# One core, cross-attention and a three-block feed-forward: first-layer weights with their output mean taken out, biases seeded into PSUM, the last layer written by token

## The chip, the core and the metric

The kernel runs on one core of one Trainium2 chip. The metric is the device time of one execution in microseconds; the time of a kernel is the median of its runs. The core has five engines that run their own queues of instructions in order and meet only at semaphores: TensorE (PE; its weight loads are listed as PEld), VectorE (DVE), ScalarE (ACT), GpSimd (POOL) and SyncE (SP, which issues the DMAs).

## The reference

`x` and `ctx` are 128 x 64 tokens of 128 features, so 8192 tokens in all. Cut to what matters:

```python
x = x + xattn(ctx, ctx, layernorm(x))        # 16 heads; softmax over the heads
h = layernorm(x)
for blk in range(3):
    i0, i1 = 2 * blk, 2 * blk + 1
    y = h @ W[i0].T + b[i0]                   # W = dequantised weights + lora_b @ lora_a
    y = (y - mean(y)) * rsqrt(var(y) + 1e-5) * gamma[blk] + beta[blk]
    y = gelu(y)
    h = y @ W[i1].T + b[i1] + h
x = x + h
```

All of it is in float32.

## The kernel before

**Two parts.** The tokens are cut into 16 chunks of 512, each four tiles of 128 tokens. The attention part walks over the chunks (`chunks`, about the first 265 us). The feed-forward part is a pipeline over the same chunks (`steps`): step `t` works on up to eight chunks at once, each at another stage. Steps 0 to 4 are placed by hand into the last chunks of the attention part (`EARLY`), steps 5 to 22 follow it; steps 8 to 13 are a loop of two steps per turn.

**Two layouts.** A first layer (`first_layer`, v = 1, 2, 3 for the three blocks) takes the transposed residual `h[v-1]` (feature by token) as weights, four tiles, and writes its output by token (token by feature), so that the mean and variance of a token lie along the free axis. A second layer takes `g[v-1]` (feature by token) and writes by feature again.

**One step, by engine.** In this order on each queue:

- PE: first layer 3 of chunk t-6 into `bank[0]`; transposes of `z[3]` of chunk t-7; first layer 2 of chunk t-4 into `bank[1]`; first layer 1 of chunk t-2 into `bank[5]` or `bank[2]`; transposes of `z[2]`, `z[1]` and of `z[0]`; second layers 3 (`bank[6]`), 2 (`bank[3]`) and 1 (`bank[4]`); transposes of `h[3]` back to by-token. Each first layer begins with `bias_rows` (L830), one bfloat16 matmul of 512 columns that writes the bias row.
- DVE: `bn_stats` of first layer 3 (L583) and `combine` of its group (group 0, with the statistics of the input chunk); `bn_stats` of first layers 2 (L591) and 1 (L595) and `combine` of group 1; `bn_stats` of the next input chunk (L570); `h[3]`, `h[2]`, `h[1]` = second layer + bias column + old h (L612, in this order); the last add into `x_all` (L618), which frees the bank and lets SP store the chunk.
- POOL: `rs2` = (variance) to the power -1/2 for group 0 and then for group 1 (L409), each followed by `nmr2` = -mean x rs (L412); then `z[0]` of chunk t in two passes (L430, L435).
- ACT: gelu of v = 3, 2, 1 (L761) on the transposed banks; `normalise(3)`, `normalise(2)` (L751, four activations of 128 columns each, from PSUM to `z[v]`); `h[0]` (L773), a copy of the transposed `z[0]`; `normalise(1)`.

`combine` (L503 to L517) has six small operations in three groups with a wait between them; `normalise` waits for `nmr2` of its group. The value that ends a step's part is its counter: `p_y[v]` first layer done, `p_st[b]` variance ready, `p_rs[b]` root ready, `p_z[v]` normalised, `p_h[v]` residual ready, `p_out` bank and chunk done.

In the start-up (chunk -1) the weights are formed as `w_eff` (L500) on DVE, transposed on PE (L823) and copied to `lin_t` on ACT (L640). Attention uses the same PSUM: `bank[4]` is `att_ps`, `bank[5]` is `wo_ps`. L557 adds the attention's output to `x_all`; one of them (chunk 14) stands on DVE's queue right behind step 4, and the bias row and the 16 matmuls of the last output projection (L830, L836 into `wo_ps`) wait for it.

## Time and profile before

| | |
|---|---|
| median of 3 runs | 407.47 us (407.38 to 407.8) |
| the profiled execution, its own time | 406.81 us |
| its span in the trace | 405.0 us |
| mean granted clock of TensorE | 0.983 |
| busy: PE / DVE / ACT / POOL | 366.2 / 351.3 / 290.1 / 288.0 us |

The profile describes one execution. The span runs from the first to the last instruction; what lies around it is 1.8 us here. Busy time on PE counts pipelined matmuls, whose ends are modelled. Instructions on DVE and ACT overlap a little: the distance from one start to the next is what an instruction costs in a queue that never waits, and its duration is what a waiting engine sees.

### The profile page before, as it was taken

The numbers are of one execution on the slowest core, as the hardware profiler recorded it, in microseconds if no ns is written. First come the engines' busy times: TensorE is split into PE (matmuls) and PEld (weight loads), VectorE is DVE, ScalarE is ACT, GpSimd is POOL, SyncE is SP. The second block draws the span as 40 slices with busy tenths as digits, with TensorE's granted clock in tenths as the row PEclk, the third lists the DMA queues.
The fourth block names the chain that finished last, engine by engine and source line by source line (L and its number), as shares of the span: only waits on it lengthen the run. The fifth ranks groups of instructions, "written<-read, shape, count | busy, mean of one in ns | idle before, by whom it ended". The sixth has DMA issues, their size and how long they took to land.

```text
span 405.0 us, 11901 instructions
## 1 busy us (share of the span) xinstructions
PE 366.2 (90%) x4205; PEld 258.1 (64%) x4205; DVE 351.3 (87%) x863; ACT 290.1 (72%) x542; POOL 288.0 (71%) x349
## 2 busy tenths in 40 slices
PE   2778999999999999999989777788999999999964
PEld 1334566677667766776656556566877887787631
DVE  4746999999999999999999999878999999888852
ACT  3447887888788878787766534358888888888741
POOL 5681998789878987898797878757667766744320
PEclk9999999999999999999999989999999999999995
DMA  5636765476547654675444100000000010001011
GB/s 164 181 105 210 218 199 150 141 235 186 159 133 221 203 159 136 201 213 163 144 133 147 39 2 2 1 2 2 28 28 26 26 52 26 28 27 53 27 53 52
DMA packets 53120, 43.26 MB, mean 107 GB/s; under 512 B 4496, under 2 KB 46944, under 8 KB 53088
## 3 DMA queue, kind: packets, MB, share of 16 engines
q1 hardware_dynamic: 53088, 42.84, 35.2%
q8 instruction: 19, 0.31, 0.3%
q14 instruction: 13, 0.11, 0.1%
HBM read 26.05 MB, written 16.78 MB: 106 GB/s over the span
## 4 chain that ended last, share of the span: by engine, by line
PE 67%; DVE 15%; POOL 7%; issue 6%; ACT 3%; DMA 1%; POOLq 0%; ACTq 0%; DVEq 0%
PE score_ps L973 8%; PE att_ps L938 7%; PE score_ps L869 7%; PE score_ps L878 6%; PE wo_ps L836 6%; PE work L1020 4%; DVE negmax L529 3%; DVE zsum L550 3%; PE score_ps L1020 3%; PE work L894 3%; PE att_ps L1020 3%; PE work L907 2%; PE score_ps L966 2%; PE score_ps L830 2%; PE work L898 2%
## 5 line engine op out<-in xcount | busy, mean ns | idle before, releaser
L373 POOL TENSOR_TENSOR probs<-probs,rz 128x1024 f32<-128x1024 f32 x64 | 136.4, 2141 | 34.0 <-DVE rz L553 33.6
L409 POOL TENSOR_TENSOR rs<-ve,minus_half 128x8 f32<-128x8 f32 (+1 forms) x40 | 55.6, 1390 | 53.4 <-DVE ve L516 53.4
L529 DVE TENSOR_REDUCE negmax<-score_ps 128x64 bf16<-128x1024 f32 x64 | 76.1, 1189 | 7.7 <-PE score_ps L869 7.6
L659 ACT ACTIVATE probs<-score_ps 128x1024 f32<-128x1024 f32 x64 | 65.6, 1025 | 23.5 <-PE score_ps L878 23.1
L550 DVE TENSOR_REDUCE zsum<-probs 128x64 f32<-128x1024 f32 x64 | 77.5, 1211 | 5.6 <-ACT probs L659 5.0
L751 ACT ACTIVATE z<-score_ps,nmr,rs 128x128 f32<-128x128 f32 x160 | 60.4, 469 | 15.3 <-POOL nmr L412 15.1
L836 PEld LDWEIGHTS wo_ps<-wo_t,att_t 128*128 128x128 f32 x256 | 37.5, 193 | 13.8 <-issue 12.2
L938 PE MATMUL att_ps<-probs,v_diag 128*32 128x64 f32 x2048 | 43.9, 225 | 1.4 <-POOL probs L373 1.4
L878 PE MATMUL score_ps<-negmax,ident_bf 128*128 128x512 bf16 x128 | 39.2, 388 | 5.6 <-DVE negmax L529 5.5
L973 PEld LDWEIGHTS score_ps<-lin_t,h 128*128 128x128 f32 x320 | 42.1, 192 | 1.3
L973 PE MATMUL score_ps<-lin_t,h 128*128 128x128 f32 x320 | 42.1, 275 | 0.0
L869 PE MATMUL score_ps<-q_stack,k_stack 128*64 128x256 f16 x512 | 40.4, 280 | 0.5 <-ACT probs L659 0.3
L938 PEld LDWEIGHTS att_ps<-probs,v_diag 128*32 128x32 f32 x2048 | 33.1, 109 | 11.5 <-issue 2.5
L836 PE MATMUL wo_ps<-wo_t,att_t 128*128 128x128 f32 x256 | 39.1, 278 | 0.0
L553 DVE RECIPROCAL rz<-zsum 128x64 f32<-128x64 f32 x64 | 35.4, 553 | 2.2
L869 PEld LDWEIGHTS score_ps<-q_stack,k_stack 128*64 128x64 f16 x512 | 23.2, 110 | 12.2 <-issue 9.7
L669 ACT ACTIVATE xln<-x_all,nmr,rstd 128x128 f32 (+1 forms) x64 | 26.2, 483 | 5.5 <-POOL rstd L399 5.5
L761 ACT ACTIVATE g<-score_ps,cols 128x512 f32<-128x512 f32 x25 | 20.0, 799 | 9.4 <-PE score_ps L966 9.4
L1020 PE MATMUL work<-g,lin_t 128*128 128x512 f32 x36 | 20.0, 638 | 3.0 <-ACT g L761 3.0
L761 ACT ACTIVATE g<-att_ps,cols 128x512 f32<-128x512 f32 x16 | 12.5, 780 | 11.5 <-PE att_ps L966 11.5
L612 DVE SCALAR_TENSOR_TENSOR h<-work,cols,h 128x512 f32<-128x512 f32 x18 | 13.4, 744 | 7.3 <-PE work L1020 7.2
L737 ACT ACTIVATE v_diag<-work 64x512 f32<-64x512 f32 x32 | 18.8, 586 | 1.1 <-PE work L907 0.7
(152 smaller groups left out, 727.6 us busy)
## 6 DMA issues: line engine op xcount, KB each, us to landing
q_parts<-parts SPq DMA_DIRECT2D x16, 512.0 KB, 3.6
q_stack<-q_parts SPq DMA_DIRECT2D x64, 128.0 KB, 2.8
k_stack<-k_parts SPq DMA_DIRECT2D x32, 256.0 KB, 3.3
ctx_sb<-in_ctx SPq DMA_DIRECT2D x16, 256.0 KB, 3.7
k_parts<-parts SPq DMA_DIRECT2D x16, 256.0 KB, 2.7
out<-x_all SPq DMA_DIRECT2D x16, 256.0 KB, 2.3
x_all<-in_x SPq DMA_DIRECT2D x14, 256.0 KB, 3.9
x_all<-in_x SPq DMA_DIRECT2D x1, 512.0 KB, 5.0
```

The lines of the kernel that those rows point to most:

```text
L373: nc.gpsimd.tensor_tensor(e[:, :, :, :], e[:, :, :, :], by_query.broadcast_to([P, BANDS, SEQ, ADJ]), ALU.mult).then_inc(s_probs, 1)
L409: nc.gpsimd.tensor_tensor(rs2[b][:, lo:hi], ve2[b][:, lo:hi], minus_half[:, lo:hi], ALU.pow).then_inc(p_rs[b], 1)
L529: nc.vector.tensor_reduce(negmax[p % 2][:, :], score_ps[p % 2][:, :].rearrange("p (h k) -> p k h", k=SEQ), AX_X, ALU.max, negate=True).the ...
L550: nc.vector.tensor_reduce(zsum[q][:, :], probs[(p - 1) % 4][:, :, :, :].rearrange("p u k s -> p k u s"), AX_XY, ALU.add).then_inc(s_zsum, 1)
L659: nc.scalar.activation(probs[p][:, :, :, :], score_ps[p % 2][:, :].rearrange("p (u s k) -> p u k s", s=ADJ, k=SEQ), ACT.Exp, scale=SCALE). ...
L751: ins = nc.scalar.activation(z[v][0][:, t, :], src[:, TILE * t:TILE * (t + 1)], ACT.Identity, bias=nmr2[b][:, lo + t:lo + t + 1], scale=rs ...
L836: ins = nc.tensor.matmul(wo_ps[:, TILE * t:TILE * (t + 1)], att[:, o, TILE * u:TILE * (u + 1)], wo_t[:, o, b, :], start=False, stop=o == 1 ...
L869: ins = nc.tensor.matmul(score_ps[mpar][SEQ * b:SEQ * (b + 1), 256 * grp:256 * (grp + 1)], k_stack[mb][:, grp, k0:k0 + SEQ], q_stack[mb][: ...
L878: ins = nc.tensor.matmul(score_ps[p % 2][:, CHUNK * o:CHUNK * (o + 1)], ident_bf[:, :], negmax[p % 2][:, :].unsqueeze(1).broadcast_to([P, ...
L938: ins = nc.tensor.matmul(att_ps[32 * grp:32 * (grp + 1), c0:c0 + SEQ], v_diag[mb][:, v0:v0 + 32], probs[mp][:, hd // ADJ, :, hd % ADJ], st ...
L973: ins = nc.tensor.matmul(dst[:, TILE * t:TILE * (t + 1)], hk[:, TILE * t:TILE * (t + 1)], lin_t[:, 2 * v - 2, :], start=False, stop=True, ...
L1020: nc.tensor.matmul(second_layer_bank(v, t), lin_t[:, 2 * v - 1, :], g[v - 1][:, :], start=True, stop=True).then_inc(p_c[v], 1)
```

## The change

Six edits, all in the feed-forward part and its start-up.

1. The first-layer weights are multiplied by `centre` (identity - 1/128) instead of being only transposed, after which the output of a first layer has no mean over its features. `normalise` needs no bias any more (`ACT.Copy` with a scale), POOL computes `nmr2` for the input chunk alone, and `combine` of group 1 has three operations with one wait instead of six with two.
2. The bias rows of layers 2 and 3 are no longer written by PE. Their centred rows stand in `seed`. ACT copies the row of layer 3 over `bank[0]` (broadcast to four tiles), DVE that of layer 2 over `bank[1]`, one step ahead, and the first layer accumulates on top.
3. The bias of first layer 1 is folded into the weights: `h[0]` is the transposed `z[0]` plus 1 (`one_col`, an activation with a bias), and row sums and bias are worked into `w_eff[0]`.
4. The bias of the last second layer travels in `h[2]` (`res_cols`).
5. The last layer is by token: PE transposes `h[2]` into `bank[6]` and accumulates `g[2]` (as weights, four tiles) x `lin_t[5]` on it; DVE adds the bank to `x_all`. `h[3]`, its DVE operation and its transposes are gone. The last add comes ahead of `h[2]` and `h[1]`.
6. Start-up: POOL makes `one_col` and `centre`; DVE works the fold into `w_eff[0]`, and forms the seeds in chunk 0 behind the first maximum (`first_layer_seeds`), for which PE writes the raw rows (`first_layer_rows`).

The core of the diff:

```diff
@@ vector @@
+            def combine(b, lo, hi, k, mean_free):
+                dve.wait_ge(p_bn[b], k + 1)
...
                 nc.vector.scalar_tensor_tensor(ag[:, 1, :], st[:, :, 2], EPS * D, st[:, :, 5], ALU.add, ALU.add)
+                if mean_free:
+                    nc.vector.tensor_tensor(ag[:, 3, :], st[:, :, 1], st[:, :, 1], ALU.mult).then_inc(p_mv[b], 1)
+                    dve.wait_ge(p_mv[b], k + 1 + (NCHUNK if b == 0 else 0))
...
+                nc.vector.scalar_tensor_tensor(ve, ag[:, 1, :], 1.0 / D, ag[:, 3, :], ALU.mult,
+                                               ALU.add).then_inc(p_st[b], 1)
...
+                if live(t - 7):
+                    dve.wait_ge(p_c[3], k + 1)
+                    nc.vector.tensor_tensor(x_all[:, k, :, :], by_token(bank[6]), x_all[:, k, :, :],
+                                            ALU.add).then_inc(p_out, 1)
+                for v, k in ((2, t - 5), (1, t - 3)):
...
+                if live(t - 3):
+                    if isinstance(t, int) and t == 3:
+                        dve.wait_ge(s_seed, 4)
+                        dve.wait_ge(s_exp, PPC * NCHUNK)
+                    if live(t - 4):
+                        dve.wait_ge(p_z[2], t - 3)
+                    nc.vector.tensor_copy(by_token(bank[1]), seed_rows(2)).then_inc(p_seed2, 1)
@@ vector, chunk 0, behind the first maximum @@
+            def first_layer_seeds():
+                nc.vector.tensor_scalar(res_cols[:, 0:1], cols[:, ROW_BL + 1:ROW_BL + 2], -1.0, None, ALU.add)
+                nc.vector.tensor_tensor(res_cols[:, 1:2], cols[:, ROW_BL + 3:ROW_BL + 4], cols[:, ROW_BL + 5:ROW_BL + 6],
+                                        ALU.add).then_inc(s_seed, 1)
+                dve.wait_ge(s_seed_ps, 1)
+                nc.vector.tensor_reduce(seed_sum[:, :], raw, AX_X, ALU.add).then_inc(s_seed, 1)
...
+                nc.vector.tensor_scalar(seed_mean[:, :], seed_sum[:, :], -1.0 / D, None, ALU.mult).then_inc(s_seed, 1)
...
+                for v in range(2):
+                    ins = nc.vector.tensor_scalar(seed[:, v, :], raw[:, v, :], seed_mean[:, v:v + 1], None, ALU.add)
@@ scalar, step t @@
                 if live(t - 6):
                     normalise(3, t - 6, 0, TPC, t + 1, bank[0])
                 if live(t - 4):
                     normalise(2, t - 4, 1, 0, t - 1, bank[1])
+                if live(t - 5):
+                    if live(t - 6):
+                        act.wait_ge(p_z[3], t - 5)
+                    nc.scalar.activation(by_token(bank[0]), seed_rows(3), ACT.Copy).then_inc(p_seed3, 1)
                 if live(t - 1):
...
-                    nc.scalar.activation(h[0][(par - 1) % 2][:, :], bank[7], ACT.Copy).then_inc(p_h[0], 1)
+                    nc.scalar.activation(h[0][(par - 1) % 2][:, :], bank[7], ACT.Identity,
+                                         bias=one_col[:, :]).then_inc(p_h[0], 1)
@@ tensor, step t, first layers (v = 3, k = t - 6; v = 2, k = t - 4; v = 1, k = t - 2) @@
                         pe.wait_ge(p_h[v - 1], k + 1)
-                        if v > 1 or (isinstance(t, int) and t <= FIRST_STEP):
-                            if some(k):
-                                pe.wait_ge(p_z[v], k)
+                        if v == 3:
+                            pe.wait_ge(p_seed3, k + 1)
+                        elif v == 2:
+                            pe.wait_ge(p_seed2, k + 1)
...
@@ tensor, last layer @@
+                    pe.wait_ge(p_h[2], k + 1)
...
+                        nc.tensor.matmul(bank[6][:, TILE * i:TILE * (i + 1)],
+                                         h[2][1 - par][:, TILE * i:TILE * (i + 1)], ident[:, :], is_transpose=True,
+                                         start=i == 0, stop=False, skip_group_check=True)
+                    pe.wait_ge(p_g[3], k + 1)
+                    for i in range(TPC):
+                        ins = nc.tensor.matmul(bank[6][:, TILE * i:TILE * (i + 1)], g[2][:, TILE * i:TILE * (i + 1)],
+                                               lin_t[:, 5, :], start=False, stop=True, skip_group_check=True)
```

## Rows read from the trace of the kernel before

**Rows 1.** Windows: busy us (instructions) of PE, PEld, DVE, ACT, POOL; PEclk; DMA; GB/s.

```profile
281.80:371.50 89.70, 89.31 (x582) 70.47 (x581) 82.27 (x341) 76.31 (x178) 58.84 (x64) 1.00 0.10 30
```

**Rows 2.** Chain that ended last, one step: start us, us, what.

```profile
306.85 0.44 PE score_ps L966 x4
307.50 0.89 PE score_ps L973 x8
...
310.81 0.86 PE work L1020 x2
```

**Rows 3.** Timeline, DVE, one step (start, duration, operation) and the next step's first.

```profile
306.89 0.89 DVE L583 BATCH_NORM_STATS2 st<-score_ps 128x6 f32<-128x128 f32 x4
...
310.46 0.21 DVE L507 TENSOR_TENSOR ag<-st 128x8 f32<-128x8 f32 x1
...
310.88 0.17 DVE L513 SCALAR_TENSOR_TENSOR ag<-ag 128x8 f32<-128x8 f32 x1
...
311.16 0.17 DVE L516 SCALAR_TENSOR_TENSOR ve<-ag 128x8 f32<-128x8 f32 x1
...
312.06 0.73 DVE L612 SCALAR_TENSOR_TENSOR h<-work,cols,h 128x512 f32<-128x512 f32 x1
...
314.44 0.68 DVE L618 TENSOR_TENSOR x_all<-wo_ps,x_all 128x512 f32 x1
...
315.04 0.89 DVE L583 BATCH_NORM_STATS2 st<-score_ps 128x6 f32<-128x128 f32 x4
```

**Rows 4.** Timeline of POOL, ACT and PE in the same step.

```profile
311.40 1.64 POOL L409 TENSOR_TENSOR rs<-ve,minus_half 128x8 f32<-128x8 f32 x1 [0.76 <-DVE ve L516]
...
313.36 1.51 ACT L751 ACTIVATE z<-score_ps,nmr,rs 128x128 f32<-128x128 f32 x4 [0.46 <-POOL nmr L412]
...
313.95 1.05 PE L973 MATMUL score_ps<-lin_t,h 128*128 128x128 f32 x8
...
314.75 0.61 ACT L773 ACTIVATE h<-work 128x512 f32<-128x512 f32 x1
```

**Rows 5.** Groups by line and form on ACT: busy us, mean ns | idle before.

```profile
L751 ACT ACTIVATE z<-score_ps,nmr,rs 128x128 f32<-128x128 f32 x160 | 60.4, 469 | 15.3 <-POOL nmr L412 15.1
...
L697 ACT ACTIVATE parts<-work,cols_h 128x512 f16<-128x512 f32 x16 | 10.9, 682 | 2.2 <-PE work L894 2.2
...
L640 ACT ACTIVATE lin_t<-att_ps 128x128 f32<-128x128 f32 x2 | 0.4, 274 | 0.0
```

**Rows 6.** Timeline, DVE in chunk 0: the second maximum.

```profile
34.73 1.22 DVE L529 TENSOR_REDUCE negmax<-score_ps 128x64 bf16<-128x1024 f32 x1 [0.54 <-PE score_ps L869]
```

**Rows 7.** Timeline, all engines, steps 4 to 6.

```profile
262.94 0.68 DVE L557 TENSOR_TENSOR x_all<-wo_ps,x_all 128x512 f32<-128x512 f32 x1
...
263.73 1.51 ACT L751 ACTIVATE z<-score_ps,nmr,rs 128x128 f32<-128x128 f32 x4 [2.67 <-POOL nmr L412]
...
263.77 0.38 PE L830 MATMUL wo_ps<-bias,pick_row 128*128 128x512 bf16 x1 [1.53 <-DVE x_all L557]
...
273.01 1.51 ACT L751 ACTIVATE z<-score_ps,nmr,rs 128x128 f32<-128x128 f32 x4 [1.99 <-POOL nmr L412]
273.70 0.89 DVE L583 BATCH_NORM_STATS2 st<-score_ps 128x6 f32<-128x128 f32 x4 [0.51 <-PE score_ps L973]
```

**Rows 8.** Timeline, PE: the same two matmuls after a long idle and without one.

```profile
241.25 1.04 PE L878 MATMUL score_ps<-negmax,ident_bf 128*128 128x512 bf16 x2 [2.61 <-DVE negmax L529]
...
244.68 0.60 PE L878 MATMUL score_ps<-negmax,ident_bf 128*128 128x512 bf16 x2
```

**Rows 9.** Timeline, steps 16 and 21, and the end.

```profile
355.75 0.89 DVE L583 BATCH_NORM_STATS2 st<-score_ps 128x6 f32<-128x128 f32 x4 [0.19 <-PE score_ps L973]
...
390.82 0.89 DVE L583 BATCH_NORM_STATS2 st<-score_ps 128x6 f32<-128x128 f32 x4 [1.49 <-PE score_ps L973]
...
392.68 1.01 POOL L409 TENSOR_TENSOR rs<-ve,minus_half 128x4 f32<-128x4 f32 x1 [4.85 <-DVE ve L516]
...
400.46 1.11 PE L1026 MATMUL wo_ps<-ident,h 128*128 128x128 f32 x4 [0.84 <-DVE h L612]
```

More of the change, by code:

```diff
@@ L106, in build @@
         lin_t = sb("lin_t", [P, NLIN, P])
+        centre = sb("centre", [P, P])
+        fold = sb("fold", [P, 3])
+        neg_last = sb("neg_last", [P, P])
+        one_col = sb("one_col", [P, 1])
+        res_cols = sb("res_cols", [P, 2])
+        seed_sum = sb("seed_sum", [P, 2])
+        seed_mean = sb("seed_mean", [P, 2])
+        seed = sb("seed", [P, 2, P])
         x_all = sb("x_all", [P, NCHUNK, TPC, D])
@@ L200, in build @@
         s_pv = sem("s_pv")
-        p_bn, p_mv, p_st, p_rs, p_nmr = ([sem(f"p_{w}{b}") for b in range(2)] for w in ("bn", "mv", "st", "rs", "nmr"))
+        p_bn, p_mv, p_st, p_rs = ([sem(f"p_{w}{b}") for b in range(2)] for w in ("bn", "mv", "st", "rs"))
+        p_nmr = sem("p_nmr")
         p_z0 = sem("p_z0_scaled")
@@ L205, in build @@
         p_zt = [sem(f"p_zt{v}") for v in range(4)]
-        p_h = [sem(f"p_h{v}") for v in range(4)]
+        p_h = [sem(f"p_h{v}") for v in range(3)]
+        p_seed2, p_seed3 = sem("p_seed2"), sem("p_seed3")
         p_g = [sem(f"p_g{v}") for v in range(4)]
@@ L265, in first_layer_bank, with by_token, seed_rows @@
             return bank[(5 if par else 2) if v == 1 else 3 - v]
-        def last_bank(par):
-            return bank[2 if par else 5]
+        def by_token(bank_ap):
+            return bank_ap.rearrange("p (t d) -> p t d", t=TPC)
+        def seed_rows(v):
+            return seed[:, v - 2, :].unsqueeze(1).broadcast_to([P, TPC, P])
         def transpose_bank(v, t, par):
@@ new lines, in feed_forward_weights @@
+                nc.vector.tensor_tensor(w_eff[:, 0, :], product_bank(0), w_deq[:, 0, :], ALU.add).then_inc(s_fold, 1)
+                nc.vector.tensor_tensor(w_eff[:, 1, :], product_bank(1), w_deq[:, 1, :], ALU.add).then_inc(s_weff, 1)
+                dve.wait_ge(s_fold, 1)
+                nc.vector.tensor_reduce(fold[:, 0:1], w_eff[:, 0, :], AX_X, ALU.add).then_inc(s_fold, 1)
+                nc.vector.tensor_tensor(w_eff[:, 2, :], product_bank(2), w_deq[:, 2, :], ALU.add).then_inc(s_weff, 1)
@@ new lines, in feed_forward_weights @@
+                dve.wait_ge(s_fold, 2)
+                dve.wait_ge(s_wready, 3)
+                nc.vector.tensor_tensor(fold[:, 1:2], cols[:, ROW_BL:ROW_BL + 1], fold[:, 0:1],
+                                        ALU.subtract).then_inc(s_fold, 1)
+                nc.vector.tensor_tensor(w_eff[:, 3, :], product_bank(3), w_deq[:, 3, :], ALU.add).then_inc(s_weff, 1)
+                dve.wait_ge(s_fold, 3)
+                nc.vector.tensor_scalar(fold[:, 2:3], fold[:, 1:2], 1.0 / D, None, ALU.mult).then_inc(s_fold, 1)
@@ L559, in chunk @@
                                                 x_all[:, c - 2, :, :], ALU.add).then_inc(s_x2, 1)
+                    if isinstance(c, int) and c == 0 and p == 0:
+                        first_layer_seeds()
                     early_steps(c, p, step)
-            def batch_stats(b, lo, hi, count):
-                combine(count - 1, p_bn[b], p_mv[b], p_nmr[b], p_st[b], st2[b][:, lo:hi, :], ag2[b][:, :, lo:hi],
-                        ve2[b][:, lo:hi], nm2[b][:, lo:hi])
             def input_stats(k):
@@ L585, in step @@
                 if live(t) or live(t - 6):
-                    batch_stats(0, 0 if live(t) else TPC, 2 * TPC if live(t - 6) else TPC, t + 1)
+                    combine(0, 0 if live(t) else TPC, 2 * TPC if live(t - 6) else TPC, t, not live(t))
                 if live(t - 4):
@@ L721, in chunk @@
                 if isinstance(c, int) and c == -1:
+                    act.wait_ge(s_wready, 3)
+                    nc.scalar.activation(neg_last[:, :], cols[:, ROW_BL + 5:ROW_BL + 6].broadcast_to([P, P]), ACT.Copy,
+                                         scale=-1.0).then_inc(s_neg_last, 1)
                     transposed_layers()
@@ L750, in normalise @@
                 for t in range(TPC):
-                    ins = nc.scalar.activation(z[v][0][:, t, :], src[:, TILE * t:TILE * (t + 1)], ACT.Identity,
-                                               bias=nmr2[b][:, lo + t:lo + t + 1], scale=rs2[b][:, lo + t:lo + t + 1])
+                    ins = nc.scalar.activation(z[v][0][:, t, :], src[:, TILE * t:TILE * (t + 1)], ACT.Copy,
+                                               scale=rs2[b][:, lo + t:lo + t + 1])
                 ins.then_inc(p_z[v], 1)
@@ L830, in bias_rows, with first_layer_rows @@
                 nc.tensor.matmul(dst, pick_row[:, which, :], src, start=True, stop=False, skip_group_check=True)
+            def first_layer_rows():
+                pe.wait_ge(s_neg_last, 1)
+                pe.wait_ge(s_lint, NLIN)
+                for v in range(2):
+                    ins = nc.tensor.matmul(att_ps[:, P * v:P * (v + 1)], pick_row[:, 3 + v, :], bias3[:, :], start=v == 0,
+                                           stop=v == 0, skip_group_check=True)
+                nc.tensor.matmul(att_ps[:, P:2 * P], neg_last[:, :], lin_t[:, 4, :], start=False, stop=True,
+                                 skip_group_check=True).then_inc(s_seed_ps, 1)
             def project_out(t, att):
@@ L881, in chunk @@
                         ins.then_inc(s_shifted, 1)
+                    if isinstance(c, int) and c == 0 and p == 0:
+                        first_layer_rows()
                     if p == 0 and live(c + 2):
```

128 lines of the change are left out of this document (69 added, 59 removed).

## The prediction, made before the changed kernel was run

> **What bounds the kernel now.** I read the windows first, then the chain that ended last, then one step of the timeline engine by engine. Between 281.8 and 371.5 us PE is busy in 89.31 of 89.70 us at the full clock [rows 1]. The chain says the same: PE's pieces follow each other with nothing between them [rows 2]. A step costs PE three first layers of 0.89, four sets of transposes of 0.44, three second layers of 0.86, the last transposes (0.44) and three bias rows of 0.21 (one of them is the stretch from 306.85 + 0.44 = 307.29 to 307.50 [rows 2]): 2.67 + 1.76 + 2.58 + 0.44 + 0.64 = 8.09 us. The period is 315.04 - 306.89 = 8.15 us [rows 3]. The reader is to see as well how little the others have left: DVE's queue is full over the whole step, start to start [rows 3], although it never shows as the bound.
>
> **The sums of the engines afterwards.** PE loses the bias rows (0.64) and the last transposes (0.44), gains the transposes of `h[2]` (0.44), and the last layer becomes four tiles (0.89) instead of two halves (0.86): 8.09 - 0.64 + 0.03 = 7.48 us. DVE loses three operations of `combine` in group 1: of the 0.70 us from its first to its last start, two waited steps of 0.20 (310.88 to 311.16 is one operation back to back, 0.08, and one waited, 0.20) become one, and 0.34 to 0.40 goes; I take 0.36. It loses `h[3]`, (314.44 - 312.06)/3 = 0.79 us, and gains the copy of the seed into `bank[1]`. No engine but PE writes PSUM in this trace, so I bound the copy by the shortest and the longest 512-column operation near it: 0.61 for a plain ACT copy [rows 4], 0.73 for DVE's three-input one [rows 3]; 0.65 is my value. DVE: 8.15 - 0.36 - 0.79 + 0.65 = 7.65 us. ACT is busy for 76.31 of 89.70 us [rows 1], gains a copy and loses bias operands; it is under 7 us. POOL loses one 0.2 us operation. Read that way, the step falls from 8.15 to about 7.65 us.
>
> The Trainium skill ("Perfetto Trace Analysis", "Identifying the Most-Contended Engine") says to take the engine with the highest occupancy and to optimise it first. The change does so, and by that rule the 7.65 us above is the result; it is the first rival below. I don't follow it, because it leaves out the new waits.
>
> **The new waits close a loop through all five queues, once per step.** ACT's copy of the seed into `bank[0]` stands behind `normalise(2)` on ACT's queue, and first layer 3 of the *next* step waits for it: step t's copy brings `p_seed3` to t-4, and at t+1 the first layer 3 (k = t-5) wants t-4. First layer 3 is the first thing that DVE waits for in a step, and DVE gets to group 1 only behind it. So, from DVE's start of L583 (zero):
>
> - DVE to `p_st[1]`: before, 306.89 to 311.16 + 0.17 = 4.44 us [rows 3]. Less 0.36 (`combine`) and less about 0.05 that L595 waits for PE in it, an estimate: 4.03.
> - POOL takes it 0.07 later and needs 1.64 for the root [rows 3, 4]: 5.74. The multiply for `nmr2` is gone from this path.
> - ACT starts `normalise(2)` 0.05 later: 5.79. It took 1.39 from its start to the next instruction (313.36 to 314.75) [rows 4], with two column operands each. One operand falls away. On 512 columns ACT takes 0.61 without such an operand [rows 4] and 0.68 with one; on 128 columns 0.469 with two and 0.274 with none [rows 5]. So one operand is 0.08 to 0.10, and four activations lose 0.34: 1.05. The seed's copy starts at 6.84.
> - The copy: 0.61, the plain copy of the same size; bounds 0.59 and 0.68 [rows 4, 5]. Done at 7.45.
> - PE: about 0.05 to see it, 0.11 for the first weights that no earlier work hides now, first layer 3 in 1.05, and 0.04 to DVE (313.95 + 1.05 = 315.00, DVE at 315.04) [rows 3, 4]: 8.70.
>
> 8.70 us is longer than any engine's sum, so this loop is the period, +0.55 against 8.15. Before, nothing tied first layer 3 to `normalise(2)`; first layer 2 waited for it, and it starts 0.89 + 0.44 + 0.21 = 1.54 us further on in PE's queue. The seed for `bank[1]` (DVE's copy behind ACT at 6.96, done 7.7) is hidden under the same wait. If the bias operand saves nothing, the period is 9.04. The Trainium skill ("ScalarE: Activation LUTs", "Step-by-step: what each stage is for") calls PSUM the faster destination for ACT than SBUF; no row here shows such a write, and the sum stands on the copy to SBUF.
>
> **Where the steps add up.** Ten steps from L583 at 273.70 to 355.75 take 82.05 us, 0.55 more than ten times 8.15 [rows 7, 9]. Afterwards 87.0 + 0.55: **+5.5**. The next five take 35.07 [rows 9]. In them group 0 has three operations too (-0.37), and in the last three the root is of four columns (1.01 instead of 1.64) [rows 9] and there is less in between; walking the same loop I get 8.3, 8.3, 7.2, 6.6 and 5.5 = 35.9: **+0.9**.
>
> **Coming into the steps.** DVE's copy in step 4 waits for ACT's `normalise(2)` of that step, and on DVE's queue the add L557 of chunk 14 stands behind it; PE's last output projection waits for that add (it already stands 1.53 us for it) and everything of step 5 behind it [rows 7]. `normalise(2)` started at 263.73; the shorter `combine` and the missing multiply (-0.55) against step 3's own copy (+0.65 less 0.2 of wait) bring it to about 263.6, its end to 264.8, the copy to 265.45. L557 moves from 262.94 to 265.4: +2.5. In step 5 the loop above applies for the first time: `normalise(2)` from 273.01 to 273.01 + 2.5 - 0.36 - 0.26 = 274.9, plus 1.05, 0.61 and 1.25: L583 at 277.8 instead of 273.70 [rows 7]: **+4.1**. PE now idles 1.53 + 2.5 = 4 us ahead of that projection. After 2.61 us of idling the same two matmuls took 1.04 instead of 0.60 us, the lower clock level [rows 8]; after 1.53 us PE was at the full one. The projection and what follows would pay about **+1.5**, from 0 to 2.
>
> **Start-up.** Most of it is hidden: POOL's two operations before the first statistics, the fold in `w_eff[0]` (some 1 us) behind PE's product for the queries. Not hidden are the seeds in chunk 0: DVE stands between the first maximum and the second (34.73, where it had 0.54 of slack [rows 6]) until PE has written the rows behind the shift, and then runs a reduction, a scalar and two operations that each wait for the last. About 2 us, of which part is caught up, since DVE is not the bound later: **+1.5**, between 0.5 and 2. The attention loop itself is untouched.
>
> **The end.** The last chunk's chain is latency: `h[3]` (0.79 with its handover, as above) and the last transposes at the low clock (1.11 + 0.04) [rows 3, 9] go, as does `nmr2` (0.26), three small operations (0.34), the bias operand (0.34). The transposes of `h[2]` are early. **-2.85**.
>
> **The sum**, against the profiled execution's 406.81: 1.5 + 4.1 + 1.5 + 5.5 + 0.9 - 2.85 = +10.6, so 417.4. The median is 0.66 above that execution: **418 us**.
>
> **Rivals.**
>
> - *The seeds are hidden* (faster). If the copy into `bank[0]` lands before PE has done its own 7.48 us, the period is DVE's 7.65: ten steps -5, the next five -1.5, the rest as above (start-up and entry +5.5 with the clock, less 0.6 for step 5, end -2.85): 403. For it: the sums. Against: the copy lands at 7.45 after DVE's start, but must land 1.25 before it, at 6.4. It decides where the copy comes a full microsecond earlier. 5%.
> - *The loop only just covers the old period.* The copy much cheaper, small handovers overlapped: 8.15 again, no loss in the steps, and the entry and the end remain: 411.5. 9%.
> - *The operand saves nothing, or the copy is dearer*: 9.04 and more, about +3.9 on 13 steps: 422. 15%.
> - *The clock falls inside the steps.* PE will idle 1.2 us in one piece per step; idle of 1.53 left it at the full level, 2.61 did not [rows 7, 8]. If it fell, first layer 3 costs 0.9 more in the loop: 430. The Trainium skill ("TensorE: Matmul & The Clock Gate", "What's actually happening") has the low level as the default that activity lifts; by that this rival follows if 86% busy is not enough. 5%.
> - The forecast: 64%, own range 415 to 421. Another 2% for something near no change.
>
> **Numbers.** The lower bounds together (start-up 0.5, no clock loss, period 8.6, 3.5 at the entry) give 412; the operand rival with upper ones 425. Range 411.5 to 425. A difference under 0.2% can't be told from none here. Faster 0.06, same 0.02, slower 0.92.
>
> **What would show it.** L583 to L583 near 8.7 us; PE idle over 1 us per step before first layer 3, ended by ACT's copy; PE no longer above 90% in those windows; `z` activations near 0.37 us; L557's second-last instance behind a DVE copy at about 265 (plus the start-up's shift); no bias rows. The prediction is wrong if first layer 3 starts without waiting for ACT, or if the period is PE's or DVE's own sum.

## The result, and the profile after

The kernel after takes 418.35 us (median of 4 runs, 417.26 to 419.26), the kernel before 407.43 us (median of 4, 405.92 to 407.8): ratio 1.0284, 95% interval 1.0253 to 1.0315. The profiled execution took 417.26 us with a span of 415.5 us, against 406.81 and 405.0 us before: +10.5 us of span. The prediction was 418 us, "slower" with 0.92. The profiled execution is the shortest of the four, at a mean granted clock of 0.988; the other three ran at 0.971 to 0.984 and took 0.7 to 2.0 us more. One run of experiment 4 took 1860 us and is left out of its median and its ratio.

The first reading is the windows over the steady steps, the view of [rows 1]. Columns: stretch, its length, busy us (instructions) of PE, PEld, DVE, ACT, POOL; granted clock; DMA share; GB/s.

```profile
286.00:373.00 87.00, 76.61 (x550) 64.44 (x549) 70.71 (x280) 64.20 (x168) 54.09 (x49) 0.98 0.10 28
```

PE was busy for all but 0.4% of the like stretch before [rows 1] and now has 12% to spare; DVE, at 81%, has not taken its place. Nobody is full, so the bound is a chain through several queues. The chain that ended last shows it (start us, us, what), the view of [rows 2]:

```profile
312.99 1.60 POOL rs L429
314.62 1.14 ACT z L810 x4
315.76 0.50 ACT score_ps L832
...
316.39 1.14 PE score_ps L1052 x8
```

Where the old chain was PE after PE, this one goes around: POOL's root, ACT's `normalise(2)`, ACT's copy of the seed into `bank[0]`, PE's first layer 3; after it come DVE's statistics (L636) and the next root. It closes once per step. The same step in the timeline (start, duration, instruction, in brackets the idle time before it and what ended it) answers to [rows 3, 4]:

```profile
317.56 0.89 DVE L636 BATCH_NORM_STATS2 st<-score_ps 128x6 f32<-128x128 f32 x4 [0.67 <-PE score_ps L1052]
...
321.36 0.17 DVE L571 SCALAR_TENSOR_TENSOR ve<-ag 128x8 f32<-128x8 f32 x1
...
321.60 1.64 POOL L429 TENSOR_TENSOR rs<-ve,minus_half 128x8 f32<-128x8 f32 x1 [0.30 <-DVE ve L571]
...
323.28 1.14 ACT L810 ACTIVATE z<-score_ps,rs 128x128 f32<-128x128 f32 x4 [0.50 <-POOL rs L429]
...
324.29 0.62 ACT L832 ACTIVATE score_ps<-seed 128x512 f32<-128x512 f32 x1
...
324.82 0.69 DVE L675 COPY score_ps<-seed 128x512 f32<-128x512 f32 x1
...
325.05 1.13 PE L1052 MATMUL score_ps<-lin_t,h 128*128 128x128 f32 x8 [0.95 <-ACT score_ps L832]
...
326.22 0.30 DVE L636 BATCH_NORM_STATS2 st<-score_ps 128x6 f32<-128x128 f32 x1 [0.71 <-PE score_ps L1052]
```

The period is 326.22 - 317.56 = 8.66 us; in the steady steps it lies between 8.60 and 8.66. PE stands 0.95 us, and what ends it is the copy L832. The waits over 290 to 375 us say how often: in us in total, times, longest.

```profile
POOL rs L429 <- DVE ve L571: 30.8, 20, 3.5
...
PE score_ps L1052 <- ACT score_ps L832: 8.0, 9, 0.9
DVE st L636 <- PE score_ps L1052: 7.8, 10, 1.9
```

POOL's 30.8 us head the list and mean nothing by themselves: POOL idles in any case, in two pieces per step. The two rows that belong together are PE's 8.0 us for ACT and DVE's 7.8 us for PE.

**Where the 10.5 us are.** The start of DVE's statistics of first layer 3 (L583, now L636) cuts the execution into parts that add up:

| part | before | after | difference | predicted |
|---|---|---|---|---|
| start-up and attention, by the third-last maximum (L529 / L584) | 239.97 | 243.16 | +3.2 | +1.5 |
| from there to L583 / L636 of step 6 | 33.73 | 38.51 | +4.8 | +5.6 |
| ten steps | 82.05 | 87.63 | +5.6 | +5.5 |
| next five | 35.07 | 36.30 | +1.2 | +0.9 |
| from there to the end of the span | 14.18 | 9.90 | -4.3 | -2.85 |
| sum | 405.0 | 415.5 | +10.5 | +10.6 |

Start-up and end are off by 1.7 and 1.4 us with opposite signs, the entry (the second row) is 0.8 below, and the ten steps hide a pair of their own. That the sum is right to 0.1 us is in part luck, since these errors cancel. Of the 5.6 us of the ten steps, the first two periods carry 1.8 (9.40 and 9.23 us, before 8.11 and 8.70) and the other eight 3.8 (69.00 us, before 65.24). The windows of the first two and of the third period show why:

```profile
281.67:291.07 9.40, 7.00 (x42) 5.49 (x41) 6.53 (x29) 6.07 (x18) 5.53 (x5) 0.90 0.01 2
291.07:300.30 9.23, 8.55 (x58) 7.27 (x57) 7.42 (x30) 5.84 (x15) 5.53 (x5) 0.91 0.10 29
300.30:308.95 8.65, 7.71 (x58) 6.43 (x57) 7.31 (x29) 6.75 (x19) 5.53 (x5) 1.00 0.11 31
```

In step 6 PE has no second layer 3 yet, so it has less to do in a loop that is as long as later. It stood 2.40 us for L832 and came back at the 1.2 GHz level (granted clock 0.54 from 289.10 to 291.07), and first layer 3, which is inside the loop, took 1.93 us:

```profile
289.11 1.93 PE L1052 MATMUL score_ps<-lin_t,h 128*128 128x128 f32 x8 [2.40 <-ACT score_ps L832]
```

**Start-up.** Here a row stands that the prediction did not have:

```profile
25.42 3.55 POOL L422 MEMSET v_diag<- 128x2048 f32 x2
...
25.97 0.28 DVE L532 TENSOR_TENSOR w_eff<-score_ps,w_deq 128x128 f32<-128x128 f32 x1
26.17 2.88 DVE L534 TENSOR_SCALAR w_eff<-w_eff,fold 128x128 f32<-128x128 f32 x1
...
29.14 0.77 PE L889 MATMUL att_ps<-centre,w_eff 128*128 128x128 f32 x2 [2.63 <-issue]
```

The last operation of the fold took 2.88 us where its neighbours of the same size took 0.28, and it ended at 29.05, together with POOL's memset (28.97). PE's products stood behind it. The first maximum (L584, the first of the maxima that DVE takes over the scores) of chunk 0 came at 34.44 instead of 32.97. Behind it are the seeds, the place of [rows 6]:

```profile
34.44 1.23 DVE L584 TENSOR_REDUCE negmax<-score_ps 128x64 bf16<-128x1024 f32 x1 [5.40 <-PE score_ps L945]
...
37.79 0.61 DVE L549 TENSOR_SCALAR seed<-att_ps,seed_mean 128x128 f32<-128x128 f32 x2
38.32 1.22 DVE L584 TENSOR_REDUCE negmax<-score_ps 128x64 bf16<-128x1024 f32 x1
```

From the first maximum to the second it takes 3.88 us instead of 1.76. Together that is 3.6 us, of which 0.4 are caught up by the third-last maximum.

**The entry**, the place of [rows 7]:

```profile
267.12 0.69 DVE L675 COPY score_ps<-seed 128x512 f32<-128x512 f32 x1 [1.45 <-ACT z L810]
267.73 0.68 DVE L612 TENSOR_TENSOR x_all<-wo_ps,x_all 128x512 f32<-128x512 f32 x1
268.56 0.42 PE L896 MATMUL wo_ps<-bias,pick_row 128*128 128x512 bf16 x1 [3.67 <-DVE x_all L612]
268.77 3.58 PE L912 MATMUL wo_ps<-wo_t,att_t 128*128 128x128 f32 x16
```

The add L612 stands behind the copy, PE idles 3.67 us (1.53 before), and its 16 matmuls take 3.58 us (1.95 before) at a granted clock of 0.55, nearly the low level.

**The end**, the place of [rows 9]. In the last 9.90 us the granted clock is 1.00; in the corresponding 14.18 us of before it was 0.63. The windows, after and then before:

```profile
405.60:415.50 9.90, 4.25 (x32) 3.40 (x30) 2.68 (x9) 2.69 (x6) 1.01 (x1) 1.00 0.19 53
```

```profile
390.82:405.00 14.18, 6.69 (x20) 2.85 (x18) 4.50 (x14) 3.06 (x6) 1.21 (x2) 0.63 0.15 46
```

### The profile page after: what moved, and what is told of

It is laid out like the page before. It is cut to its first block, busy times and chain, and to the rows that moved or that the text cites. A ratio compares the mean times of both kernels' runs of the same rounds, so it can differ in the third digit from the quotient of the medians.

```text
span 415.5 us, 11911 instructions
## 1 busy us (share of the span) xinstructions
PE 359.6 (87%) x4260; PEld 262.5 (63%) x4260; DVE 345.7 (83%) x801; ACT 283.7 (68%) x559; POOL 283.3 (68%) x327
## 4 chain that ended last, share of the span: by engine, by line
PE 46%; DVE 22%; POOL 13%; issue 9%; ACT 8%; DMA 1%; POOLq 0%; DVEq 0%; ACTq 0%
PE att_ps L1018 7%; POOL rs L429 7%; PE score_ps L945 6%; PE score_ps L954 6%; PE wo_ps L912 6%; PE score_ps L1052 5%; ACT z L810 5%; DVE negmax L584 3%; DVE zsum L605 3%; DVE st L636 2%; PE work L972 2%; PE work L985 2%; DVE st L644 2%; DVE st L648 2%; DVE ag L558 2%
## 5 line engine op out<-in xcount | busy, mean ns | idle before, releaser
L584 DVE TENSOR_REDUCE negmax<-score_ps 128x64 bf16<-128x1024 f32 x64 | 76.1, 1189 | 5.8 <-PE score_ps L945 5.7
L1052 PE MATMUL score_ps<-lin_t,h 128*128 128x128 f32 x320 | 43.9, 285 | 18.7 <-ACT score_ps L832 17.8
L1052 PEld LDWEIGHTS score_ps<-lin_t,h 128*128 128x128 f32 x320 | 39.5, 197 | 32.0 <-DVE h L667 22.7
L810 ACT ACTIVATE z<-score_ps,rs 128x128 f32<-128x128 f32 x160 | 45.5, 375 | 12.1 <-POOL rs L429 12.1
L912 PEld LDWEIGHTS wo_ps<-wo_t,att_t 128*128 128x128 f32 x256 | 39.0, 201 | 13.8 <-issue 12.2
L912 PE MATMUL wo_ps<-wo_t,att_t 128*128 128x128 f32 x256 | 40.7, 287 | 0.0
L636 DVE BATCH_NORM_STATS2 st<-score_ps 128x6 f32<-128x128 f32 x64 | 14.3, 285 | 14.3 <-PE score_ps L1052 14.3
L659 DVE TENSOR_TENSOR x_all<-work,x_all 128x512 f32<-128x512 f32 (+1 forms) x16 | 11.1, 692 | 12.2 <-PE work L1110 12.2
L954 PEld LDWEIGHTS score_ps<-negmax,ident_bf 128*128 128x128 bf16 x128 | 7.3, 97 | 19.9 <-issue 11.1
```

What stands on the lines that cost most here:

```text
L584: nc.vector.tensor_reduce(negmax[p % 2][:, :], score_ps[p % 2][:, :].rearrange("p (h k) -> p k h", k=SEQ), AX_X, ALU.max, negate=True).the ...
L810: ins = nc.scalar.activation(z[v][0][:, t, :], src[:, TILE * t:TILE * (t + 1)], ACT.Copy, scale=rs2[b][:, lo + t:lo + t + 1])
L912: ins = nc.tensor.matmul(wo_ps[:, TILE * t:TILE * (t + 1)], att[:, o, TILE * u:TILE * (u + 1)], wo_t[:, o, b, :], start=False, stop=o == 1 ...
L954: ins = nc.tensor.matmul(score_ps[p % 2][:, CHUNK * o:CHUNK * (o + 1)], ident_bf[:, :], negmax[p % 2][:, :].unsqueeze(1).broadcast_to([P, ...
L1052: ins = nc.tensor.matmul(dst[:, TILE * t:TILE * (t + 1)], hk[:, TILE * t:TILE * (t + 1)], lin_t[:, 2 * v - 2, :], start=v == 1 and t == 0, ...
```

## The experiments

Eight kernels ran, in two groups of four; each group shares its runs of the kernel before (406.69 us, 13 runs; 405.61 us, 12 runs). Each edit is against the kernel after unless it says otherwise. Periods and starts are those of `bn_stats` of first layer 3. The kernel after was measured beside a third set of runs of before (407.43 us); so where two kernels are compared across groups, their ratios to before are compared and not their times.

### 1. The seed's copy ahead of `normalise(2)`

```diff
                     normalise(3, t - 6, 0, TPC, t + 1, bank[0])
-                if live(t - 4):
-                    normalise(2, t - 4, 1, 0, t - 1, bank[1])
                 if live(t - 5):
...
                     nc.scalar.activation(by_token(bank[0]), seed_rows(3), ACT.Copy).then_inc(p_seed3, 1)
+                if live(t - 4):
+                    normalise(2, t - 4, 1, 0, t - 1, bank[1])
```

> The changed kernel with ScalarE's copy of the seed into bank[0] moved ahead of normalise(2) on its queue; nothing else. Loop theory: the copy leaves the path through the second root; the step is then set by DVE's own copy behind normalise(2), 4.02 + 0.05 + 1.64 + 0.06 + 1.14 + 0.13 + 0.7 = about 7.75 us instead of 8.63, ten steps -8.8, the next five -3 to -4, the total near 406. Rival (the copy only takes ScalarE's time, wherever it stands): the period stays at 8.6 and the total at 418.

Measured: 405.82 us (10 runs, 404.57 to 407.17), ratio 0.9982 (0.9958 to 1.0005). Against the kernel after (1.0284) that is 2.9% less time, for the order of two statements on one queue. The period is 7.93 us, PE is busy in all 70 us of the window from 290 to 360:

```profile
290.00:360.00 70.00, 70.00 (x495) 57.00 (x496) 62.39 (x255) 57.61 (x151) 48.91 (x45) 1.00 0.12 32
```

and first layer 3 starts with no wait, the copy done 0.76 us before it (ACT and PE in one step):

```profile
310.75 0.60 ACT L830 ACTIVATE score_ps<-seed 128x512 f32<-128x512 f32 x1
311.28 1.12 ACT L810 ACTIVATE z<-score_ps,rs 128x128 f32<-128x128 f32 x4
312.11 1.16 PE L1052 MATMUL score_ps<-lin_t,h 128*128 128x128 f32 x8
```

So the loop through `normalise(2)` is what made the steps slow, and it is opened here: expected were a period of 7.75 us and a total near 406. Ten steps take 78.88 us (before 82.05), the next five 33.78 (35.07), the end 9.83 (14.18): 8.8 us gained. Start-up and entry cost 8.4 us (step 6 begins at 282.11 instead of 273.70) and eat it. The chain of a step is now PE after PE. It is 0.45 us longer than the 7.48 of the prediction: from its start to PE's next piece first layer 3 takes 1.15 us and not 0.89, and first layer 2 costs 1.09, because it starts only behind DVE's copy into `bank[1]` (done at 313.52, first layer 2 from 313.67). That copy, hidden under the loop before, is the next thing in the way.

### 2. The add of chunk 14 ahead of step 4's copy

```diff
                                                 x_all[:, c - 2, :, :], ALU.add).then_inc(s_x2, 1)
+                    if isinstance(c, int) and c == NCHUNK and p == 3:
+                        dve.wait_ge(p_z[2], 1)
+                        nc.vector.tensor_copy(by_token(bank[1]), seed_rows(2)).then_inc(p_seed2, 1)
...
-                    nc.vector.tensor_copy(by_token(bank[1]), seed_rows(2)).then_inc(p_seed2, 1)
+                    if not isinstance(t, int) or t != 4:
+                        nc.vector.tensor_copy(by_token(bank[1]), seed_rows(2)).then_inc(p_seed2, 1)
```

> The changed kernel with step 4's DVE copy of the seed placed behind the add of chunk 14 into x_all, instead of ahead of it. Queue theory: that add starts 1.9 us earlier, PE idles 1.7 instead of 3.7 us and does its 16 matmuls in 1.95 instead of 3.58 us; -3.5 us in all, the total near 415. Rival (step 5 waits for something else, POOL or ACT): within 1 us of 418.

Measured: 415.6 us (4 runs, 412.86 to 416.02), ratio 1.0197 (1.0145 to 1.0248), 0.87% or 3.5 us under the kernel after; the two intervals miss each other by only 0.0005. The profile is plain on the place:

```profile
268.16 0.68 DVE L612 TENSOR_TENSOR x_all<-wo_ps,x_all 128x512 f32<-128x512 f32 x1
...
268.99 0.38 PE L900 MATMUL wo_ps<-bias,pick_row 128*128 128x512 bf16 x1 [1.53 <-DVE x_all L612]
269.20 1.95 PE L916 MATMUL wo_ps<-wo_t,att_t 128*128 128x128 f32 x16
```

PE's idle time is back at the 1.53 us of [rows 7], and the 16 matmuls take 1.95 us instead of 3.58. (L612 is not earlier in absolute time: this execution is 1.1 us behind at the third-last maximum, 244.30 against 243.16, and 2.6 us behind at step 3's copy, 261.85 against 259.29. Experiment 5 shows the rows of that stretch.) Step 6 begins at 280.48 instead of 281.67, 2.3 us earlier when the 1.1 is counted; without the delay before step 3's copy it would be more. The period stays 8.61 to 8.63: entry and loop are separate costs.

### 3. The last operation of the fold reads PSUM

```diff
-                nc.vector.tensor_scalar(w_eff[:, 0, :], w_eff[:, 0, :], fold[:, 2:3], None,
-                                        ALU.add).then_inc(s_weff, 1)
+                nc.vector.scalar_tensor_tensor(w_eff[:, 0, :], product_bank(0), fold[:, 2:3], w_deq[:, 0, :],
+                                               ALU.add, ALU.add).then_inc(s_weff, 1)
```

It computes the same sum from the product that is still in PSUM, in place of the copy of it in SBUF.

> The changed kernel with the last operation of the fold written as product (PSUM) + column + dequantised weights in one operation, instead of a tensor_scalar from SBUF to SBUF that took 2.88 us beside GpSimd's 3.55 us memset. Port theory (that operation waited for the memset to end): it takes about 0.3 us, the first scores come 1.5 to 1.7 us earlier, the total is near 416.7. Rival (code fetch or another first-use cost): it still takes over 2 us and nothing moves.

Measured: 416.56 us (4 runs, 416.39 to 416.74), ratio 1.0242 (1.0204 to 1.0281); the intervals overlap, so by the times alone the gain of 0.4% isn't shown. The rows show what it is made of (POOL, then DVE):

```profile
25.43 3.55 POOL L422 MEMSET v_diag<- 128x2048 f32 x2
```

```profile
26.19 0.34 DVE L534 SCALAR_TENSOR_TENSOR w_eff<-score_ps,fold,w_deq 128x128 f32<-128x128 f32 x1
```

The same memset runs, at the same place, and the operation takes 0.34 us instead of 2.88. The first maximum comes at 32.10 instead of 34.44, and that is 0.9 us before the 32.97 of the kernel before: without the hold-up the fold is hidden, as predicted. At the third-last maximum the 2.4 us are still there (240.79 against 243.16). At step 6 only 0.6 us are left (281.05): the entry gave back the rest, at a lower clock (experiment 5).

### 4. A bias column for `normalise` again

```diff
-                    ins = nc.scalar.activation(z[v][0][:, t, :], src[:, TILE * t:TILE * (t + 1)], ACT.Copy,
-                                               scale=rs2[b][:, lo + t:lo + t + 1])
+                    ins = nc.scalar.activation(z[v][0][:, t, :], src[:, TILE * t:TILE * (t + 1)], ACT.Identity,
+                                               bias=zero_col[:, :], scale=rs2[b][:, lo + t:lo + t + 1])
```

> The changed kernel with a column of zeros as bias operand in normalise, so two column operands per activation as in the kernel before. Loop theory: 4 x 0.085 to 0.093 = 0.34 to 0.37 us more per step on the loop, 8.63 to about 8.98, 13 steps +4.5, the total near 423. Rival (ScalarE has slack, over 1 us idle per step): no change, 418.

Measured: 427.72 us (3 runs, 426.53 to 428.88), ratio 1.0517 (1.0456 to 1.0577). The period is 8.96 to 9.02 where 8.98 was expected, and PE's wait in the loop grows from 0.95 to 1.25 us. In the steady steps (ACT and PE):

```profile
337.11 1.50 ACT L812 ACTIVATE z<-score_ps,zero_col,rs 128x128 f32<-128x128 f32 x4 [0.16 <-POOL rs L431]
...
339.24 1.13 PE L1054 MATMUL score_ps<-lin_t,h 128*128 128x128 f32 x8 [1.25 <-ACT score_ps L834]
```

The total is nearly 5 us above the expectation, which priced the period alone. Against the kernel after, step 6 begins 2.5 us later (284.19), of which 2.0 were there before the entry, and the end takes 11.0 us instead of 9.9, at a granted clock of 0.75 and not 1.00. The first two periods take 9.90 and 10.38 us, 0.9 more than the operand accounts for, at a granted clock of 0.84 (0.90 and 0.91 there): PE is at the low level for longer, in first layers that are inside the loop.

### 5. The seeds' start-up work divided and moved

The reduction and its scaling go behind the second maximum on DVE, the two subtractions to ACT, and `res_cols` is formed in the weight part.

```diff
-                ins = nc.vector.tensor_scalar(seed[:, v, :], raw[:, v, :], seed_mean[:, v:v + 1], None, ALU.add)
...
+                        ins = nc.scalar.activation(seed[:, v, :], att_ps[:, P * v:P * (v + 1)], ACT.Identity,
+                                                   bias=seed_mean[:, v:v + 1])
```

> The changed kernel with the start-up seeds formed otherwise: the residual columns in the weight part, the reduction and the mean on DVE behind the second maximum instead of the first, the two subtractions on ScalarE. DVE then pays about 0.6 us in chunk 0 instead of 2.1: the second maximum 2.1 us earlier against the first, the total -1.5, near 417. Rival (the start-up shift is caught up anyway): 418.

Measured: 418.37 us (4 runs), ratio 1.0301 (1.0273 to 1.033): no gain against 1.0284. The second maximum now follows the first after 1.77 us, as before the change (1.76); the third gives 0.5 of the 2.1 us back. The rest holds: from the first maximum to the third-last it takes 207.17 us, against 208.72 in the kernel after, 1.55 less. In this execution the first maximum came late, at 35.20, and the entry took 40.28 us instead of 38.51, so that step 6 begins at 282.65. The entry's extra time goes with a lower clock. The 7.70 us behind the add of chunk 13 (L612), in the kernel after and then in this one:

```profile
251.59:259.29 7.70, 6.49 (x119) 5.23 (x123) 6.94 (x23) 2.16 (x3) 6.57 (x6) 1.00 0.01 2
```

```profile
250.79:258.49 7.70, 6.49 (x90) 5.60 (x91) 6.36 (x21) 2.16 (x3) 5.59 (x5) 0.78 0.01 2
```

A first layer in this stretch took 1.16 us in the kernel after and 1.97 in experiment 3, and step 3's copy came 16.13 us behind the third-last maximum in the kernel after and 17.61 here. From the last L612 to step 6 it took 9.29 us in the kernel after, at a granted clock of 1.00, and 10.73 here, at 0.76. Experiment 3 has the same three numbers (0.78, 0.76, 10.73) and an entry of 40.26. Experiments 1, 2 and 8 have the 0.78 as well; only experiments 4 and 7 are at 1.00 there like the kernel after. What lowers the clock in that stretch no run separates.

### 6. The kernel before without the bias rows

Edit against the kernel **before**. It leaves out the biases of all first layers.

```diff
-                bias_rows(dst, 1 + v)
                 for t in range(TPC):
                     ins = nc.tensor.matmul(dst[:, TILE * t:TILE * (t + 1)], hk[:, TILE * t:TILE * (t + 1)],
-                                           lin_t[:, 2 * v - 2, :], start=False, stop=True, skip_group_check=True)
+                                           lin_t[:, 2 * v - 2, :], start=t == 0, stop=True, skip_group_check=True)
```

> The kernel before without the three bias rows of the first layers (the first-layer biases are left out of the computation). PE's sum falls from 8.09 to 7.45 us per step. PE-only theory: period 7.5, ten steps -6.5, total near 398. Full-queue theory (DVE's queue is full at 8.15 start to start, though it never shows as the bound): the period falls by 0.1 to 0.2 at most, the total 405 to 407.

Measured: 402.44 us (4 runs, 400.6 to 403.77), ratio 0.993 (0.9904 to 0.9957). The period is 7.91 us: 0.64 us less of PE's work gave 0.24, a little more than the 0.1 to 0.2 of the second theory, and the total lies below its 405 to 407: ten steps took 78.94 us (-3.1), the next five 34.15 (-0.9), and the end 12.34 (-1.8, which is the clock, as the end of the next section shows). The chain that ended last now goes through DVE, from one L583 to the next:

```profile
305.45 0.88 DVE st L583 x4
...
307.99 0.80 DVE st L595 x4
...
310.38 0.75 DVE h L612
...
312.75 0.54 DVE x_all L618
313.35 0.89 DVE st L583 x4
```

DVE's queue, which never showed as the bound in the profile before, stood 0.24 us behind it. A seed that lands on DVE has to be set against that.

### 7. Only the seeding undone

PE writes the bias rows of layers 2 and 3 again (the rows as they are, without their mean taken out; that is the difference in what is computed). Everything else of the change stays.

```diff
+                if v > 1:
+                    bias_rows(dst, 1 + v)
...
-                    nc.scalar.activation(by_token(bank[0]), seed_rows(3), ACT.Copy).then_inc(p_seed3, 1)
...
-                    nc.vector.tensor_copy(by_token(bank[1]), seed_rows(2)).then_inc(p_seed2, 1)
```

> The changed kernel with the seeding of bank[0] and bank[1] undone alone: no copies by ScalarE and DVE, PE writes the bias rows of layers 2 and 3 again as one matmul each (not centred: the means of these two biases are left in). PE's sum is 7.48 + 0.43 = 7.9 us, DVE's about 7.0. Loop theory: the loop is gone, PE is the bound at 7.9 to 8.0, ten steps -6.8, entry -3.5, the total near 404 to 406. Rival (the step is slow for the token order of the last layer): period stays near 8.6.

Measured: 402.87 us (5 runs, 401.71 to 404.64), ratio 0.9941 (0.9914 to 0.9969). So the other edits together are worth -0.6%, and the seeding alone takes the kernel from 0.9941 to 1.0284. The rival, that the last layer by token makes the step slow, would have kept the period near 8.6 and is out. Here PE is the bound (69.81 us busy of 70.00), the period 8.07 to 8.13 (7.9 to 8.0 was expected), and step 6 begins at 276.45 us, 5.2 us earlier than in the kernel after: the copy in front of the add of chunk 14 and the wait for the copy in step 5 are gone. The start-up's loss is still there (third-last maximum at 243.49).

### 8. All seeds on ACT, with the right order

Edits 1, 3 and 5 together, and the copy into `bank[1]` on ACT's queue behind `normalise(2)`, off DVE's:

```diff
-                    nc.vector.tensor_copy(by_token(bank[1]), seed_rows(2)).then_inc(p_seed2, 1)
...
                     nc.scalar.activation(by_token(bank[0]), seed_rows(3), ACT.Copy).then_inc(p_seed3, 1)
+                if live(t - 4):
+                    normalise(2, t - 4, 1, 0, t - 1, bank[1])
+                if live(t - 3):
...
+                    nc.scalar.activation(by_token(bank[1]), seed_rows(2), ACT.Copy).then_inc(p_seed2, 1)
```

> All repairs together: seed of bank[0] ahead of normalise(2), seed of bank[1] on ScalarE behind it instead of on DVE, the fold through PSUM, the start-up seeds split. Theory: no loop longer than PE's sum remains, period 7.5 to 7.65, ten steps -10 to -11 against the changed kernel, the next five -3.5, entry -3.5, start-up -3: total near 398. Rival (another ring of waits near 8 us takes over): 402 to 405.

Measured: 396.54 us (6 runs, 394.46 to 397.69), ratio 0.9759 (0.9732 to 0.9787): 2.4% under before and 5.1% under the kernel after. Step 6 begins at 273.77 us, as in the kernel before (273.70); ten steps take 77.8 us (-4.2), five 33.3 (-1.8), the end 11.01 (-3.2). The start-up's 3.2 us are gone (third-last maximum at 239.58), and of the entry's 4.8 us 0.5 are left. PE is the bound without a gap:

```profile
290.00:360.00 70.00, 70.00 (x511) 58.37 (x510) 58.85 (x245) 64.18 (x165) 46.87 (x42) 1.00 0.12 35
```

The period is 7.73 us where PE's sum was worked out as 7.48 (and 7.5 to 7.65 was expected). What experiment 2 moved has no copy in front of it any more. PE's timeline shows most of the difference: first layer 3 costs 0.99 us to the next start instead of 0.89 (its weights are `h[2]`, for which the weight loads wait 0.8 us per step), and in front of it the second layer takes 0.58 us to the next start instead of 0.43:

```profile
311.17 0.59 PE L1121 MATMUL att_ps<-g,lin_t 128*128 128x512 f32 x1
311.75 1.16 PE L1055 MATMUL score_ps<-lin_t,h 128*128 128x128 f32 x8
312.74 0.60 PE L1049 MATMUL score_ps<-ident,z 128*128 128x128 f32 x4
```

## Why the prediction was right, step by step

**The mechanism was right, and it is shown.** The claim was a loop DVE, POOL, ACT, PE, DVE that closes because the copy into `bank[0]` stands behind `normalise(2)` on ACT's queue and the next step's first layer 3 waits for it. The waits of the kernel after name that pair, and experiment 1 opens the loop with nothing but the order on that queue: 8.63 to 7.93 us. Experiment 4 stretches the one link by 0.36 us and the period follows by the same. Of the signs that were named, PE's idle came out at 0.95 us and not over 1. The sizes, from DVE's start of L636:

| link | predicted | measured |
|---|---|---|
| DVE to `p_st[1]` | 4.03 | 3.97 |
| POOL's root done (start + 1.64) | 5.74 | 5.68 |
| `normalise(2)` starts, to the seed's copy | 5.79, 1.05 | 5.72, 1.01 |
| the copy, PSUM written by ACT | 0.61 | 0.62 |
| from the copy's end over PE to DVE's next start | 1.25 | 1.31 |
| period | 8.70 | 8.66 (mean 8.63) |

(DVE's copy, bounded between 0.61 and 0.73 and taken as 0.65, is 0.69.) In the rivals and bounds two sums slip without touching the forecast: 0.34 us on 13 steps are 4.4 and not 3.9, and the lower bounds add up to about 414 (407.47 + 0.5 + 3.5 + 4.5 + 0.9 - 2.85) and not 412. The bias operand's price came out as worked out from [rows 5]: 469 ns before, 375 ns now by the group,

```profile
L810 ACT ACTIVATE z<-score_ps,rs 128x128 f32<-128x128 f32 x160 | 45.5, 375 | 12.1 <-POOL rs L429 12.1
```

and 465 ns in experiment 4. The Trainium skill ("ScalarE: Activation LUTs", "What ACT_TABLE_LOAD costs") gives about 93 ns for each such pointer operand; these runs show 94 and 90.

**The rule of the busiest engine did not hold.** The Trainium skill ("Perfetto Trace Analysis", "Identifying the Most-Contended Engine") has the engine with the highest occupancy optimised first, though it says that matmul busy time is no good measure of TensorE's headroom and that the weight loads' busy share is one to take instead; here that was 79% (70.47 of 89.70 us), with DVE busy for 92%. By busy time PE came first, at 99.6%. PE's busy time per step fell from 8.11 (89.31 of 89.70, times 8.15) to 7.6 us (76.61 of 87.00, times 8.63), and the period rose to 8.63, because the work was not removed but handed to two queues whose turn came later. Once the copy is in its right place PE is without a gap again, and the period comes near its sum (7.93 and 7.73 against 7.48, experiments 1 and 8).

**Start-up: mis-sized, +3.2 us instead of +1.5.** Two costs were priced. The seeds in chunk 0 ("about 2 us") measured 2.1 between the first two maxima. The fold ("some 1 us, behind PE's product for the queries") was taken as hidden, and this is the term that failed: its last operation was held up by POOL's memset, and the first maximum came 1.5 us late. Experiment 3 takes the hold-up away, and the first maximum comes at 32.10. Behind the maxima 0.4 us were caught up.

**Entry: +4.8 us instead of +5.6.** The mechanism is the one named, the add of chunk 14 behind step 4's copy, and PE's idle of "4 us" was 3.67; experiment 2 takes it away alone. The clock's part was put at 1.5 us, and the 16 matmuls show 1.63 (3.58 against 1.95). So the shift without the clock is 3.2 us, 0.9 less than the 4.1 predicted. The difference lies ahead of the add: with the start-up's 3.19 taken off, `normalise(2)` of step 4 starts at 262.76 and not at 263.6, and the add moves by 1.6 us, not 2.5. All this holds for the profiled execution; where the clock is at 0.78 in the entry (experiments 3 and 5) the same part is 6.5 us longer than before.

**Ten steps: +5.6 us instead of +5.5, by two errors that cancel.** The loop added 0.47 us a step in the eight steady periods and not 0.55, which makes 0.6 us less. And the rival "the clock falls inside the steps", which had 5%, came true in one step of the fifteen: in step 6 PE idled 2.40 us, not 1.2, as it has no second layer 3 yet. The two periods took 18.63 us, 1.4 more than two at 8.63; the prediction had them like the others, with 0.55 on top for all ten.

**The end: mis-sized, -4.3 us instead of -2.85.** The clock is what was missing. Experiment 6 separates the two, as its last chunk has the same chain as before at nearly the full level:

```profile
386.46:398.80 12.34, 4.62 (x20) 2.02 (x18) 4.50 (x14) 3.06 (x6) 1.21 (x2) 0.97 0.17 55
```

From 12.34 to 9.90 is the structure, -2.4. From 14.18 (clock 0.63) to 12.34 is the clock, -1.8. The predicted terms, with the transposes at the 0.66 + 0.04 us that they take in experiment 6 instead of 1.11 + 0.04, make -2.4 as well. So the structure was right, and the prediction priced the low level only for the transposes that vanish, not for the second layer (2.07 us in the kernel before at that level, 1.13 in experiment 6) and the `z` transposes (1.11 against 0.66). That the end would run at the full level it did not say. Whether the clock holds to the end is not given by the code alone: the kernel of experiment 8 has the end of the kernel after and took 11.01 us at 0.83.

**What stays open.** Why the clock behind the add of chunk 13 was 1.00 in the profiled executions of the kernel after and of experiments 4 and 7, and 0.78 in the others. And experiments 2 and 3 measured less than 1% each on runs whose intervals nearly touch or overlap; for them the rows of the trace carry the verdict, and experiment 8 the sum.

## What to carry to other kernels

Work that is taken off a full engine lands at a place in another queue: write down what stands in front of it there and who waits for it in the *next* step, since the kernel stood at 1.028 with the copy behind one statement and at 0.998 with it ahead. Where no engine is full, add up the links of the loop from the durations in the trace; it gave the period to 0.07 us. Look separately at the steps that enter and leave a pipeline, in which the busiest engine has less to do and idles longest, because there the clock takes its share.

## What the runs showed of the hardware

**DVE held while POOL works.** The fold's last operation reads and writes SBUF and took 2.88 us beside POOL's memset; in the executions of experiments 1, 2, 4 and 5 the same code took 3.38 to 3.40 and in experiment 7 it took 2.89, and each time it ended with the memset, less than 0.1 us behind it. As another operation with an operand from PSUM it took 0.34 (experiment 3). A first use of the operation is not the cause, as a `tensor_scalar` on one column (L530) took 0.14 just before. No run took the memset away: that it is the holder rests on the ends that coincide. The kernel before has the like in another place; DVE and then POOL there:

```profile
251.51 1.47 DVE L507 TENSOR_TENSOR ag<-st 128x4 f32<-128x4 f32 x1
```

```profile
248.58 4.39 POOL L373 TENSOR_TENSOR probs<-probs,rz 128x1024 f32<-128x1024 f32 x2 [0.66 <-DVE rz L553]
```

L507, on four columns, took 1.47 us and ended at 252.98; POOL's passes ended at 252.97. The Trainium skill ("SBUF — State Buffer", "SBUF: two separate sides") calls the ports that DVE and GpSimd share an exclusive lock, held for the whole instruction, for DVE operations in a two-port mode or, against a GpSimd operation that reads SBUF, with two SBUF inputs; these durations agree with that.

**The clock after idle time.** The same 16 output-projection matmuls took 1.95 us after 1.53 us of idle and 3.58 after 3.67; first layer 3 took 1.13 us after 0.95 of idle and 1.93 after 2.40. The length of the idle stretch alone doesn't give the price: after 3.41 us in experiments 3 and 5 the 16 matmuls took 2.65 and 2.68. In experiment 4, after 2.11 us, first layer 3 still began at the full level (1.13) and the *next* first layer took 1.91. A wait's price can come one or two instructions after the wait.
